# Two halves of a residual addition on two engines, in a chain of four small transformer layers

## The reference

```
xn = (x - mean(x)) / sqrt(var(x) + eps)      # over the 128 features of a token
xm = xn * scale + shift
y  = attention(xm) @ Wproj                   # blocks 0 and 4
y  = gelu(xm @ W1 + b1) @ W2                 # blocks 1, 2, 3 and 5 (hidden width 512, 128, 256, 512)
x  = x + gate * (y + bias)
```

## Time and profile before

| what | value |
|---|---|
| median of 3 runs | 567.05 us |
| the profiled execution | 570.62 us |
| its span in the profile | 568.7 us |
| granted TensorE clock, mean | 0.954 |
| busy: TensorE, VectorE, ScalarE, GpSimd | 476.4, 429.7, 383.0, 392.8 us |
| the residual addition L682 | 48 times, 60.7 us busy |
| the statistics' first instruction L956 | 192 times, 41.4 us busy |

### The profile page before, as it was taken

One profiled execution on the slowest core, in us unless ns is written; L12 is line 12 of the kernel. 1 busy time (PEld: TensorE's weight loads), 2 busy tenths in 40 slices (PEclk: granted clock), 3 DMA queues, 4 the chain that ended last, 5 costly groups with the idle time before them and its releaser, 6 DMA issues.

```text
span 568.7 us, 21089 instructions
## 1 busy us (share of the span) xinstructions
PE 476.4 (84%) x9062; PEld 324.6 (57%) x9062; DVE 429.7 (76%) x914; ACT 383.0 (67%) x633; POOL 392.8 (69%) x408
## 2 busy tenths in 40 slices
PE   5877686898899789888899988767899988887996
PEld 2445354566557566465566555455576665565674
DVE  5888899899728856966899967898995454688841
ACT  7895375657587848666796836745866656686961
POOL 2768666667567879559887848655649899755546
PEclk9989898999599969999999987998999999899999
DMA  8514134123042620451433330212344232153321
GB/s 290 194 42 159 60 85 117 47 77 97 9 106 76 199 82 1 117 147 56 128 100 108 111 86 23 68 39 61 112 122 111 75 82 69 28 139 89 94 78 75
DMA packets 23468, 53.43 MB, mean 94 GB/s; under 512 B 5840, under 2 KB 8144, under 8 KB 23376
## 3 DMA queue, kind: packets, MB, share of 16 engines
q1 hardware_dynamic: 22912, 51.14, 31.5%
q10 hardware_dynamic: 432, 0.94, 0.4%
q0 software_dynamic: 32, 0.01, 0.1%
HBM read 39.74 MB, written 2.88 MB: 75 GB/s over the span
## 4 chain that ended last, share of the span: by engine, by line
POOL 27%; DVE 24%; PE 24%; issue 11%; ACT 6%; DMA 4%; SPq 4%; POOLq 0%; DVEq 0%; ACTq 0%
POOL x L682 5%; PE work L1169 5%; POOL x L678 4%; POOL rstd L672 4%; PE work L1178 4%; POOL xm L689 4%; DVE prob L932 4%; PE work L1128 4%; DVE mx L925 3%; POOL kbd L656 3%; POOL prob L667 2%; SPq L580 2%; PE work L1101 2%; DVE prob L927 2%; PE work L1048 2%
## 5 line engine op out<-in xcount | busy, mean ns | idle before, releaser
L793 ACT ACTIVATE xn<-x,nmr,rstd 128x128 f32<-128x128 f32 x192 | 78.5, 482 | 41.4 <-POOL nmr L675 41.3
L1169 PE MATMUL work<-xm,w_layer 128*128 128x512 f32 x176 | 91.5, 634 | 10.4 <-POOL xm L689 9.7
L1178 PEld LDWEIGHTS work<-w_layer,prob 128*128 128x128 f32 x704 | 83.0, 195 | 12.8 <-ACT prob L798 8.7
L1178 PE MATMUL work<-w_layer,prob 128*128 128x128 f32 x704 | 86.8, 280 | 2.3 <-ACT prob L798 2.2
L798 ACT ACTIVATE prob<-work,first 128x512 f32<-128x512 f32 x88 | 58.7, 684 | 42.7 <-PE work L1169 42.5
L678 POOL TENSOR_TENSOR x<-x,q_gate 128x512 f32<-128x512 f32 x48 | 60.8, 1273 | 31.7 <-DMA q_gate<-gates_out 31.7
L932 DVE STREAM_TRANSPOSE prob<-prob 128x1024 f32<-128x1024 f32 x64 | 78.4, 1232 | 2.5 <-ACT prob L784 2.5
L682 POOL TENSOR_TENSOR x<-x,q_gate 128x512 f32<-128x512 f32 x48 | 60.7, 1271 | 24.1 <-DVE q_gate L971 24.0
L689 POOL TENSOR_TENSOR xm<-turned_in,mod 128x512 f32<-128x512 f32 x48 | 50.6, 1056 | 30.1 <-DVE turned_in L966 30.1
L1128 PE MATMUL work<-vbd,prob 128*32 128x36 f32 x4096 | 52.6, 208 | 21.8 <-issue 10.2
L1128 PEld LDWEIGHTS work<-vbd,prob 128*32 128x32 f32 x4096 | 46.1, 117 | 41.1 <-issue 27.2
(11 more groups left out here) (138 smaller groups left out, 933.9 us busy)
## 6 DMA issues: line engine op xcount, KB each, us to landing
q_gate<-gates_out SPq DMA_DIRECT2D x192, 128.0 KB, 2.9
vbd<-v_ev SPq DMA_DIRECT2D x128, 72.0 KB, 2.4
kbd<-in_adj SPq DMA_DIRECT2D x8, 704.0 KB, 5.0
turned_in<-in_x_tok SPq DMA_DIRECT2D x8, 256.0 KB, 3.0
out_x<-x SPq DMA_DIRECT2D x8, 256.0 KB, 2.2
turned_in<-in_x_feat SPq DMA_DIRECT2D x7, 256.0 KB, 4.5
w_layer<-in_weights SPq DMA_DIRECT2D x2, 768.0 KB, 5.3
w_layer<-in_modw SPq DMA_DIRECT2D x1, 768.0 KB, 7.4
```

The source lines that it names most:

```text
L793: act.activation(xn[s][:, t], x[s][:, t], ACT.Identity, scale=rstd[s][:, t:t + 1], bias=nmr[s][:, t:t + 1]).then_inc(xn_ready[s], 1)
L1169: pe.matmul(bank(s, f"h{j}.{u}"), w[UP[j]][:, 0, u * D:(u + 1) * D], xm[s][:], start=True, stop=True).then_inc(filled[s], 1)
L1178: last = pe.matmul(bank(s, f"y{a}")[:, t * D:(t + 1) * D], hT[s][u][:, t * P:(t + 1) * P], w[DOWN[a]][:, u], start=(u == 0 and t == 0), st ...
```

## The change

The product's semaphore `y_ready` counts two signals a block instead of one. VectorE, right behind its product, waits for its own product and for GpSimd's bias, adds tokens 2 and 3 of the product to x and signals `y_ready` again. GpSimd's residual adds tokens 0 and 1 only and waits for the first of the two signals; it still signals `x_ready`. Who needs x waits for both. The statistics take tokens 2 and 3 first, behind VectorE's own signal, and wait for `x_ready` only ahead of token 0. All five orders in `MERGE` are others: the same stages, at other places. The helpers `add_shift` and `await_xm` hold code that stood in the stages before and issue the same instructions.

```diff
+HALF = 2
 MERGE = {
-    "tensor": ("001020420142012402044200420402042230011321302020103303221113013010120323112032000020123213212130"
+    "tensor": ("001024024104021240420204020040421230023123102200103303221103103102130021312032000203012311212201"
...
-    "vector": ("000142201204041202400204200032030012012132203210320321021013120110310321122120323303210231110213"
+    "vector": ("004012214024010022004402200033020012102312221030302302321012111010310321123210233023120211023131"
...
-    "gpsimd": ("120201020232104044203012010323123321102002010132103102020302131031001300122021201231231231220133"
+    "gpsimd": ("120210023022100444203012012031332320121002010313101202020203130311031000222101201232121323012132"
...
         def await_x(eng, c, j):
             if j:
                 eng.wait_ge(x_ready[c % NS], count(c, NBLK, j))
+                eng.wait_ge(y_ready[c % NS], count(c, 2 * NBLK, 2 * j))
...
-            READ[f"y{j_}"] = (y_ready, NBLK, j_ + 1)
+            READ[f"y{j_}"] = (y_ready, 2 * NBLK, 2 * j_ + 1)
...
+        def add_shift(eng, s, a, c, part):
+            shift = mod[:, 2 * a + 1, c * NB:(c + 1) * NB].rearrange("p (t b) -> p t b", b=BT)
+            turned_out = keys_order(xm[s][:]) if BLOCKS[a][0] == "attn" else as_seqs(xm[s][:])
+            scaled_x = as_seqs(xm0[s][:])[:, part]
+            return eng.tensor_tensor(turned_out[:, part], scaled_x, shift[:, part].unsqueeze(3).broadcast_to(scaled_x.shape), ALU.add)
+
+        def await_xm(eng, c, j):
+            eng.wait_ge(xm_ready[c % NS], count(c, NBLK, j + 1))
...
                 if kind == "residual":
-                    pool.wait_ge(y_ready[s], count(c, NBLK, a + 1))
+                    pool.wait_ge(y_ready[s], count(c, 2 * NBLK, 2 * a + 1))
                     pool.wait_ge(biased[s], count(c, NBLK, a + 1))
-                    pool.tensor_tensor(x[s][:], x[s][:], qT[s], ALU.add).then_inc(x_ready[s], 1)
+                    pool.tensor_tensor(x[s][:, 0:HALF], x[s][:, 0:HALF], qT[s][:, 0:HALF], ALU.add).then_inc(x_ready[s], 1)
...
                 if kind == "stats":
-                    await_x(dve, c, a)
-                    for t in range(T):
+                    tokens = [*range(HALF, T), *range(HALF)]
+                    if a:
+                        chain(y_ready, 2 * NBLK, 2 * a)
+                    else:
+                        await_x(dve, c, a)
+                    for t in tokens:
+                        if a and t == 0:
+                            dve.wait_ge(x_ready[s], count(c, NBLK, a))
                         dve.bn_stats(stats[s][:, t], x[s][:, t]).then_inc(dve_step[s], 1)
-                    for t in range(T):
-                        dve.wait_ge(dve_step[s], count(c, OWN_STEPS, OWN["stats", a] - T + t + 1))
+                    for k, t in enumerate(tokens):
+                        dve.wait_ge(dve_step[s], count(c, OWN_STEPS, OWN["stats", a] - T + k + 1))
                         dve.bn_aggr(mv[s][:, t], stats[s][:, t]).then_inc(dve_step[s], 1)
...
                     dve.tensor_tensor(gate[s], bank(s, f"y{a}").rearrange("p (t f) -> p t f", f=D), gate[s], ALU.mult
                                       ).then_inc(y_ready[s], 1)
+                    chain(y_ready, 2 * NBLK, 2 * a + 1)
+                    dve.wait_ge(biased[s], count(c, NBLK, a + 1))
+                    dve.tensor_tensor(x[s][:, HALF:T], x[s][:, HALF:T], qT[s][:, HALF:T], ALU.add).then_inc(y_ready[s], 1)
```

More of the change, by code:

```diff
@@ L180 @@
-    "gpsimd": ("120201020232104044203012010323123321102002010132103102020302131031001300122021201231231231220133"
[L181 to L184, removed]
+    "tensor": ("001024024104021240420204020040421230023123102200103303221103103102131021312032000203012311212201"
+               "300231121231303221001301121301203032023103121202302013033112132321021120100312032320230113031002"
+               "301222203232303120320203131201231301210123122313231230233130232311311313120133323131322032301202"
+               "121231032103231221321012330130311111320333321310012003013231112232033103120131313231021300021103"
+               "3203132021102121301300323030223022000002"),
@@ new lines @@
+    "vector": ("004012214024010022004402200033020012102312221030302302321012111010310321123210233023120211023131"
+               "303110100322303123130212302301013022100210103130221232123311023201222331010320102313310332023301"
+               "301223302021222332101200122313131231013133331321122312332022310021113013311303120330231120133112"
+               "3210233013120213303210111301330032101322123230223000020001032"),
+    "scalar": ("444044040421442400200142242044204310121020330131033230112020002012331120102123102310301221013123"
+               "002103120232103211303231211302203001123320103022322103030320231211321223210103133321233131123033"
+               "311232320120123120301312223123103111130233133102030012311322013302131133102300231021320011231100"
+               "233032302000220"),
@@ L185 @@
+    "gpsimd": ("120210023022100444203012012031332320121002010313101202020203130311031000222101201232121323012132"
+               "210100231012313013330320231223202331012310321012123230331302311232310231230313212303110313122233"
+               "21121301023302131120211330311232310132302131202133031302030201003101103322230200021030312"),
+    "sync": ("020044224100133103220111023230102301032011122302220331123001233213113332210312301201331203103132"
+               "21030201302"),
 }
@@ L587, in stage @@
                 if kind == "next_x":
-                    sp.wait_ge(xm_ready[s], count(c, NBLK, NBLK))
+                    await_xm(sp, c, NBLK - 1)
                     load_x(c + NS)
@@ L686, in stage @@
                         await_mod(pool, a)
[L687 to L690, removed]
+                    add_shift(pool, s, a, c, slice(0, T)).then_inc(xm_ready[s], 1)
             for kind, a, c in ORDERS["gpsimd"]:
@@ L1041, in stage @@
                     if a >= 2:
-                        pe.wait_ge(xm_ready[s], count(c, NBLK, 1 if a == 2 else 5))
+                        await_xm(pe, c, 0 if a == 2 else 4)
                     if c < NS and a == 0:
@@ L1163, in stage @@
                     if u == 0:
-                        pe.wait_ge(xm_ready[s], count(c, NBLK, j + 1))
+                        await_xm(pe, c, j)
                         if c < NS and j == 2:
```

## The result

The changed kernel took 570.4 us (median of 19 runs, 568.38 to 573.18) beside 568.54 us for the kernel before on the same chips: a ratio of 1.0043, interval 1.0022 to 1.0064. It is 0.4% slower, 2.4 us. The forecast was 0.6% faster. They leave out runs more than 1.5% above the fastest of their kernel, so a ratio can differ from that of the medians of all runs, here by up to 0.6%; where that matters, the ratio of medians is given too. For the changed kernel it is 1.0033. The experiments ran on three chips, each beside the kernel before.

The account below looks back on a forecast made before the run. No single engine was taken to set the time; GpSimd's residual addition was the chain's costliest line. The terms -13.3 + 5.1 + 6.5 - 1.7 = -3.4 us gave 567.2 us profiled, 563.7 us by median runs; range 553 to 575.

Parts of the forecast that it names:

- (a): GpSimd's residual addition cut from 512 to 256 elements: 0.58 us less each, 13.3 us off the chain (12.2 to 14.5).
- R3: Rival, no change: the shorter addition uncovers what runs beside it, such as TensorE; 566 to 568 us, chance 0.18.
- (b): VectorE's 48 new half additions with both inputs in SBUF: 0.41 us each, occupying VectorE 0.33, 16 us in all.
- (c): The two halves exclude each other on SBUF reads: VectorE's queue stands 20 us, GpSimd's holds add 5.1 us.
- (d): VectorE's added work on the path, 36 us of additions and holds: costs 6.5 us at the end (3.8 to 14.6).
- (e): Statistics of tokens 2 and 3 first, out from behind GpSimd's half: gains 1.7 us (nothing to 9.9).
- (f): VectorE's new wait in its queue for GpSimd's bias: costed at nothing, 3.5 us if uncovered at 8 places.
- (g): The new stage orders and extra semaphore checks: cost taken as nothing, 4 us either side for the orders.
- The marks: Signs to check: durations of both halves, GpSimd's and VectorE's busy times, L682's chain share, VectorE's idle time before statistics.
- R1: Rival, room for both: VectorE's half falls into gaps of GpSimd and nothing holds; 555.9 us, chance 0.17.
- R2: Rival, slower: VectorE's in-order queue is held behind GpSimd's instructions at the new addition; 574.2 us, chance 0.29.
- the chain's mark: Sign that the residual addition L682 would fall well under 5.1% of the chain.

## Why the prediction was wrong

The ratios in the old orders make a ladder: before 1, the shorter addition 0.9869, early statistics and their waits 0.9829, VectorE's half without the hold 0.9943, with it 1.0032; the new orders then 1.0043. In microseconds: -7.4, -2.3, +6.5, +5.1, +0.6, in all +2.4. The steps of 2.3 and 0.6 are within the intervals; the others are outside them or just so. By medians the same steps are -9.3, +0.2, +5.7, +4.5 and +0.6 us: the same shape, with no gain from the early statistics.

- (a) is the step that failed: it paid all 23 additions of the chain in full. Each addition did get shorter by 0.54 us (0.58 said), but 7.4 us came of it at the end (3.5 to 11.3), not 13.3, and its lower bound of 12.2 was too high too. The chain shows one path; only 12 of its 23 whole additions were still on it once they were short. After the others something else ended last, TensorE's work by its share, which is argued. R3 had named this mechanism, with a chance of 0.18, and no part of it went into the sum. With 7.4 in place of 13.3 the sum of the prediction is +2.5 us, and 2.4 was measured. That it fits to 0.1 us is luck: with the 9.3 us of the medians it would be +0.6, where the medians have +1.9.
- (b) was right: 0.42 us alone, 0.41 said; VectorE's busy time rises by 15.3 us with the unheld half (446.3 against 431.0 us in the old orders), 16 said.
- (c) had the mechanism right, and the sizes off the two ways. VectorE was held (0.599 - 0.421) x 48 = 8.5 us, not 20. Its half started inside a GpSimd instruction in 23 of 48 places, where the prediction had 28 of 45 product ends, and it was stretched in only 15 of the 23, by 0.57 us on average. In five it ended inside L683, the power, which I had counted as holding and which held nothing (before, the same power, L672, covered 5 of the 28); in the other three GpSimd's instruction was nearly over. GpSimd was held (0.895 - 0.728) x 48 = 8.0 us where 17/45 x 48 x 0.33 = 6 was said: by 0.24 or 0.19 each time instead of 0.33, but more often, since VectorE goes first even after a wait. By the Trainium skill, "SBUF — State Buffer", section "Who interferes with whom", the operand's place decides; the halves at 728 and 421 ns with one operand in PSUM agree with it. That the second instruction waits until the first is done, as the prediction took it, the trace doesn't bear out everywhere: VectorE's half ran in 0.42 us inside the 1.01 us of L683, and GpSimd's half lost 0.24 us to VectorE's 0.42. Where they differ, the measurement decides.
- (c) and (d) together were put at 11.6 us for VectorE's half with its holds. From 0.9829 to 1.0032 it is 11.5. That the sum fits is luck in part and doesn't make each price right: 16 us of own time cost 6.5 us at the end, 0.4 per us and not VectorE's 24% of the chain, and the held microseconds, 8.5 and 8.0 instead of 20 and 6, cost 5.1.
- (e) 1.7 us said; 2.3, not told from nothing. (f) at nothing: right, VectorE waited 3.6 us in all for the bias. (g) at nothing: right as far as the runs tell. In four pairs of kernels, new orders and old, none of the differences is outside the intervals (1.0043 and 1.0032, 0.9964 and 0.9943, 0.9951 and 0.9942, 0.9882 and 0.9829), and by medians two of the four lie the other way (0.9902 and 0.9942, 0.9931 and 0.9940). The eight table loads that they added weren't in the prediction; they could have been counted in ScalarE's order, 49 changes of function against 41.
- The marks: VectorE's half at a mean of 0.60 (near 0.8 said) lay between R1's 0.45 and R2's 0.91, as in the forecast; GpSimd's minimum was under 0.9, VectorE's busy time 462 (468 said), GpSimd's 374 (371 said). Only the chain's mark spoke against it: 4.2% is not well under 5.1%. The others tested the durations, and the sign hung on the price of (a) at the end.

## What to carry to other kernels

Don't take a line's share of the chain as what shortening it gives: here 7.4 of 13.3 us came, with TensorE 84% busy beside it, since about half of the additions left the chain. Cut such an instruction by itself in one run, even if the result is then incomplete; the sign hung on this one price. When work is split between VectorE and GpSimd, let VectorE's part have one operand in PSUM, even at the price of one more instruction: the same split went from 1.0043 to 0.9951. Orders laid out for one duration can hurt with another: on the whole addition the new ones cost 3.8%, while on the split the old ones did as well as the new.

## What the runs showed of the hardware that was not expected

- GpSimd's L683, a power over 4 elements of 1.02 us, doesn't hold a VectorE instruction with two SBUF inputs: at 466.64 and in four more places VectorE's half keeps its 0.42 to 0.43 inside it. GpSimd's other instructions that met it, over 256 to 1408 elements, hold it to their end: the held halves end 0.27 to 0.29 us after them.
- When VectorE is held and GpSimd's next instruction is ready too, VectorE goes first: at 192.71, and in nine more places where a GpSimd half follows a held VectorE half, GpSimd's takes 0.90 to 0.92 instead of 0.72.
- GpSimd's addition costs 0.20 us at 4, 0.73 at 256 and 1.27 at 512 elements: a straight line of 2.1 ns for each element and 0.19 us fixed.
- Eight more loads of a function table, 1.28 us each, on an engine busy 69% of the span, cost nothing that twelve runs could tell.
